# A selective scan in a twelve-stage decoder: four batches one after another, against four prepared in bulk and 64 states in one sequence

## The reference, cut to what matters

```python
xi = silu(conv3(u @ Win + b_in))            # depthwise convolution over time, three taps
z  = silu(u @ Wg + bg)
dt = softplus(xi @ Wdt + bdt)               # B=4, T=512, D=128
Bm, Cm = xi @ Wb + bb, xi @ Wc + bc         # 16 states
dA  = exp(dt[..., None] * A)
dBx = dt[..., None] * Bm[:, :, None, :] * xi[..., None]
h_t = dA_t * h_{t-1} + dBx_t                # for each batch, channel, state
y_t = sum over states of h_t * C_t
out = (y * z) @ Wout + bout                 # added to the residual x
```

## Time and profile before

| | us |
|---|---|
| median of 3 runs | 3147.62 (3141.78 to 3148.28) |
| profiled execution | 3148.16, its span 3146.4 |
| PE, DVE, ACT, POOL busy | 2411.6, 1811.8, 1239.4, 534.3 |
| the phase `l1_attn` in the span | 449.4 to 706.8 |

### The profile page before, as it was taken

How to read it: one execution, slowest core, us unless ns; L and a number is a source line. 1 busy time by engine, 2 the same in 40 slices (tenths; PEclk the granted TensorE clock), 3 DMA queues, 4 the chain that set the end, 5 groups by cost and what they waited for, 6 DMA issues and landing times. The chain is left out here.

```text
span 3146.4 us, 40958 instructions
## 1 busy us (share of the span) xinstructions
PE 2411.6 (77%) x12416; PEld 1417.6 (45%) x12416; DVE 1811.8 (58%) x4431; ACT 1239.4 (39%) x2575; POOL 534.3 (17%) x509
## 2 busy tenths in 40 slices
PE   6763976666768998699688888775888879578587
PEld 4653642224623323366344444453444456557454
DVE  4666347778855576444544444345666643745777
ACT  2442342224344454322466666523444422223212
POOL 0410000003310000000455555342000000043100
PEclk7875977777879999799799999877999989688799
DMA  0000000001010000000322222000000000100000
GB/s 32 31 6 0 1 5 0 0 0 44 1 55 1 0 0 0 0 0 0 97 69 68 68 68 68 22 31 24 1 0 0 0 1 0 56 23 1 1 1 14
DMA packets 19876, 61.81 MB, mean 20 GB/s; under 512 B 4928, under 2 KB 4928, under 8 KB 18592
## 3 DMA queue, kind: packets, MB, share of 16 engines
q1 hardware_dynamic: 19488, 59.53, 6.0%
q10 hardware_dynamic: 256, 0.68, 0.1%
HBM read 42.37 MB, written 1.05 MB: 14 GB/s over the span
## 5 line engine op out<-in xcount | busy, mean ns | idle before, releaser
L689 DVE TENSOR_REDUCE MF<-P 128x1 f32<-128x512 f32 (+3 forms) x512 | 282.3, 587 | 97.4 <-PE P L479 53.3
L824 ACT ACTIVATE PT<-P 128x512 f32<-128x512 f32 (+3 forms) x512 | 244.2, 516 | 232.5 <-PE P L496 123.0
L2318 PE MATMUL P<-XT,W 128*128 x424 | 221.0, 618 | 63.4 <-ACTq L2352 63.4
L2394 DVE SCALAR_TENSOR_TENSOR X<-P,WE,X 128x128 f32 x576 | 162.5, 344 | 167.0 <-PE P L2335 162.0
L2335 PEld LDWEIGHTS P<-W,e_h 128*128 128x128 f32 (+1 forms) x1952 | 220.7, 191 | 61.1 <-issue 53.2
L2335 PE MATMUL P<-W,e_h 128*128 128x128 f32 (+1 forms) x1952 | 227.8, 278 | 3.3 <-DVE X L2394 3.3
L1286 POOL TENSOR_TENSOR d_e<-d_e,d_rc 128x512 f32<-128x512 f32 (+3 forms) x256 | 178.2, 723 | 223.1 <-DVE d_rc L1193 223.0
L2363 ACT ACTIVATE e_g<-P 128x512 f32<-128x512 f32 x148 | 88.4, 597 | 310.5 <-PE P L2318 310.5
L496 PE MATMUL P<-QA,KA 128*128 128x512 bf16 (+3 forms) x512 | 180.2, 358 | 32.6 <-ACT PT L824 12.7
L479 PE MATMUL P<-KA,QA 128*128 128x512 bf16 (+3 forms) x512 | 182.2, 362 | 28.3 <-ACT KA L808 15.1
L541 PE MATMUL P<-PT,VA 128*32 128x512 f32 (+3 forms) x1024 | 195.8, 518 | 0.0
(11 more groups left out here) (359 smaller groups left out, 4635.5 us busy)
## 6 DMA issues: line engine op xcount, KB each, us to landing
d_bt<-in_alibi SPq DMA_DIRECT2D x32, 512.0 KB, 3.7
d_moved<-d_raw SPq DMA_DIRECT2D x256, 64.0 KB, 2.0
W<-in_w_L_xattn SPq DMA_DIRECT2D x1, 4291.0 KB, 14.1
W<-in_w_L_ffn SPq DMA_DIRECT2D x1, 3333.0 KB, 11.1
W<-in_w_L_ffn SPq DMA_DIRECT2D x1, 3155.0 KB, 10.2
W<-in_w_L_attn SPq DMA_DIRECT2D x1, 2636.0 KB, 11.6
W<-in_w_L_ffn SPq DMA_DIRECT2D x1, 2310.0 KB, 9.0
W<-in_w_L_ffn SPq DMA_DIRECT2D x1, 1744.0 KB, 6.9
```

The lines of the kernel that those rows point to most:

```text
L689: last = v.tensor_reduce(col, src, AX.X, ALU.max, negate=True)
L824: a.activation(k.PT[0:self.kp, h % self.slots, t, N - w:N], src, ACT.Exp, scale=self.scale).then_inc(s("exp_done"), 1)
L2318: pe.matmul(P[:, PG + j % 2, :], w["w1"][:, col:col + 128], x, start=True, stop=True).then_inc(s("gate"), 1)
L2394: last = v.scalar_tensor_tensor(x, y, k.WE[:, bass.ds(c * 4 + t, 1), e], x, ALU.mult, ALU.add)
```

## The change: what it does

Nothing outside `l1_attn` changes but the packing of `bout`, which becomes a row repeated over the 128 partitions. In the phase:

- The loop over batches is gone; every buffer of the preparation has one part per batch, and the four batches are prepared stage by stage before the first state.
- The bias and copy of the first product move from DVE to ACT (`conv_in`). dt and dt*x move from DVE to GpSimd (`delta`). `bout` is added to all of `X` at once by GpSimd; the products with ones are gone.
- The 64 states (16 of each batch) are one sequence. The product `inp` is split: ACT copies the spread B row with its bias from PSUM to `BE`, and GpSimd multiplies `BE` by dt*x into `BX`. DVE keeps the scan and `out`.
- `DA` gets three parts. B rows are spread two states ahead of C rows.
- The product with z comes 4 states after the last one of its batch, the product with Wout after 6, the addition to `X` after 9; the sum over states has two PSUM banks in turn.

The core of the diff (removed lines are those printed above):

```diff
+            def add_state(m):
+                b, n = m // NS, m % NS
+                pe.wait_ge(s("hc"), m + 1)
...
+                pe.matmul(P[:, BANK_Y + b % 2, :], k.ident[:], HC[:, m % 2, :], start=n == 0, stop=n == NS - 1).then_inc(s("summed"), 1)
...
+            for m in range(ALLS + AFTER_OUT + 1):
+                if m + 2 < ALLS:
+                    b_row(m + 2)
+                if m < ALLS:
+                    c_row(m)
+                if 0 <= m - 2 < ALLS:
+                    add_state(m - 2)
+                if m >= AFTER_OUT and (m - AFTER_OUT) % NS == 0 and m >= NS:
+                    out((m - AFTER_OUT) // NS - 1)
 
         @block.scalar
...
+            def b_row(m):
+                a.wait_ge(s("b_full"), m + 1)
+                if m >= 2:
+                    a.wait_ge(s("bx"), m - 1)
+                a.activation(BE[:, m % 2, :], P[:, BANK_B + m % 2, :], ACT.Identity, bias=w["bb"][:, m % NS:m % NS + 1]).then_inc(s("be"), 1)
+
+            def decay(m):
+                if m % NS == 0:
+                    a.wait_ge(s("dt"), m // NS + 1)
+                if m >= 3:
+                    a.wait_ge(s("scan"), m - 2)
+                a.activation(DA[:, m % 3, :], DT[:, m // NS, :], ACT.Exp, scale=w["a"][:, m % NS:m % NS + 1]).then_inc(s("da"), 1)
...
+            for b in range(B):
+                delta(b)
+            for m in range(ALLS):
+                b_row(m)
+                decay(m)
+
+        @block.gpsimd
+        def _(g):
...
+            g.tensor_tensor(k.X[:], k.X[:], w["bout"].unsqueeze(1).to_broadcast([128, TILES, D]), ALU.add).then_inc(s("offset"), 1)
+
+            def delta(b):
+                g.wait_ge(s("re"), b + 1)
+                g.wait_ge(s("ab"), 2 * b + 2)
+                g.tensor_tensor(DT[:, b, :], RE[:, b, :], AB[:, b, :], ALU.add).then_inc(s("dt"), 1)
+                g.wait_ge(s("dt"), b + 1)
+                g.tensor_tensor(DTX[:, b, :], DT[:, b, :], XS[:, b, :], ALU.mult).then_inc(s("dtx"), 1)
+
+            for b in range(B):
+                delta(b)
+            g.wait_ge(s("dtx"), B)
+            for m in range(ALLS):
+                g.wait_ge(s("be"), m + 1)
+                if m >= 2:
+                    g.wait_ge(s("scan"), m - 1)
+                g.tensor_tensor(BX[:, m % 2, :], BE[:, m % 2, :], DTX[:, m // NS, :], ALU.mult).then_inc(s("bx"), 1)
 
         @block.vector
...
+            def scan(m):
+                v.wait_ge(s("da"), m + 1)
+                v.wait_ge(s("bx"), m + 1)
+                if m >= 2:
+                    v.wait_ge(s("hc"), m - 1)
+                v.tensor_tensor_scan(H[:, m % 2, :], DA[:, m % 3, :], BX[:, m % 2, :], 0.0, ALU.mult, ALU.add).then_inc(s("scan"), 1)
+
+            def out(m):
+                v.wait_ge(s("c_full"), m + 1)
+                v.wait_ge(s("scan"), m + 1)
+                if m >= 2:
+                    v.wait_ge(s("summed"), m - 1)
+                v.scalar_tensor_tensor(HC[:, m % 2, :], P[:, BANK_C + m % 2, :], w["bc"][:, m % NS:m % NS + 1], H[:, m % 2, :],
+                                       ALU.add, ALU.mult).then_inc(s("hc"), 1)
...
+            for m in range(ALLS + AFTER_ADD + 1):
+                if m < ALLS:
+                    scan(m)
+                if 0 <= m - 1 < ALLS:
+                    out(m - 1)
+                if m >= NS and m % NS == AFTER_Z:
+                    gated(m // NS - 1)
+                if m >= NS and m % NS == AFTER_ADD:
+                    add(m // NS - 1)
```

More of the change, by code:

```diff
@@ L1975, in _ @@
             w_ready(pe)
[L1976 to L1981, removed]
-                pe.wait_ge(s("xs"), b + 1)
[L1983 to L2003, removed]
@@ L2004, in _, with out @@
+            def out(b):
                 pe.wait_ge(s("yz"), b + 1)
-                pe.wait_ge(s("m_free"), 3 * b + 3)
+                if b == 0:
+                    pe.wait_ge(s("rest"), B)
+                else:
+                    pe.wait_ge(s("added"), b)
                 for t in range(QT):
-                    o = P[:, PM, 128 * t:128 * (t + 1)]
-                    pe.matmul(o, YZ[:, 128 * t:128 * (t + 1)], w["wout"], start=True, stop=False)
-                    last = pe.matmul(o, k.ones[0:1, 0:128], w["bout"], start=False, stop=True)
@@ L2010, in _ @@
-                last.then_inc(s("m_full"), 1)
+                    last = pe.matmul(P[:, BANK_OUT, 128 * t:128 * (t + 1)], YZ[:, b % 2, 128 * t:128 * (t + 1)], w["wout"], start=True, stop=True)
+                last.then_inc(s("out_full"), 1)
+            conv_in(0)
+            conv_in(1)
+            gate(0)
+            gate(1)
+            conv_in(2)
+            conv_in(3)
+            delta(0)
+            gate(2)
+            gate(3)
+            delta(1)
+            rows(0)
+            rows(1)
@@ L2014, in _, with conv_in @@
             w_ready(a)
-            a.sem_inc(s("z_free"), 1)
-            with a.Fori(0, B) as b:
-                a.wait_ge(s("conv"), b + 1)
[L2018 to L2022, removed]
+            def conv_in(b):
+                a.wait_ge(s("in_full"), b + 1)
+                if b == 0:
+                    a.wait_ge(s("edges"), 1)
+                a.activation(XC[:, b, 1:N + 1], P[:, BANK_A + b % 2, :], ACT.Identity, bias=w["bin"]).then_inc(s("xc"), 1)
@@ L2023, in _ @@
                 a.wait_ge(s("abs"), b + 1)
-                a.activation(AB[:], AB[:], ACT.Exp, scale=-1.0).then_inc(s("ab"), 1)
+                a.activation(AB[:, b, :], AB[:, b, :], ACT.Exp, scale=-1.0).then_inc(s("ab"), 1)
                 a.wait_ge(s("ab"), 2 * b + 1)
[L2026 to L2030, removed]
+                a.activation(AB[:, b, :], AB[:, b, :], ACT.Ln, bias=1.0).then_inc(s("ab"), 1)
@@ L2034, in _ @@
             w_ready(v)
[L2035 to L2043, removed]
@@ new lines, in _ @@
+            for b in range(B):
+                conv(b)
+            for b in range(2):
+                positive(b)
+            for b in range(2):
+                rows(b)
+            for b in range(2, B):
+                positive(b)
+            for b in range(2, B):
+                rows(b)
+            for m in range(ALLS + AFTER_ADD + 1):
[7 more added lines that the diff above has]
+                    add(m // NS - 1)
```

184 lines of the change are left out of this document (120 added, 64 removed).

## The result

The kernel after takes 3098.36 us (median of 4 runs, 3087.09 to 3098.92) against 3145.76 (4 runs, 3141.78 to 3148.28): ratio 0.9839, 95% interval 0.9816 to 0.9862. A second set gave 3094.02 (5 runs, 3087.2 to 3098.48) against 3149.24, ratio 0.9825 (0.9811 to 0.9839). Forecast were 3092 and a range of 3068 to 3106: faster, and in the range.

A forecast was written before the change was run, and what follows sets the result against it. Bound per state: GpSimd's product and DVE's scan in turn. First scan's end 490.0, 63 periods of 2.43 (153.1), insertions 1, tail 6.4 end the phase at 650.5, 56.3 us less than 3148.16: 3092 us, range 3068 to 3106.

The forecast's parts named there:

- The clash: In the states: DVE's scan, with two SBUF inputs, and GpSimd's product exclude each other, so the scan waits.
- The period: Time per state in the sequence: 2.43 us against 2.63 before; chance 0.70 for 2.35 to 2.6.
- the hand-over: Between a scan's end and the start of GpSimd's next product: 0.08 us per state.
- the scan's rest: What the waiting scan still takes after GpSimd's product ends: 1.08 us per state.
- The preparation: Work ahead of the states, once instead of four times: first scan ends at 490.0, about 41 us into the phase.
- The insertions: Three products with z and three additions inside the sequence, mostly under the wait for GpSimd: 1 us in all.
- The tail: From the last scan to the end of the last addition: 6.4 us, against 8.6 before.
- PE: About 2.55 us per state at 1.2 GHz, half at 2.4; nothing taken, 8 us if all states ran low.
- The shared scan: Rival in the states: scan runs beside GpSimd's product, 1.99 us per state, 3066 us (halfway 2.2, 3077); chance 0.17.
- A held `out`: Rival in the states: `out` also waits for GpSimd, period 2.87 us, 3120 us; chance 0.10, shared with a dearer product.
- The full relay: Rival in the states: scan, `out` and product all wait in turn, 3.9 us per state, 3184 us; chance 0.03.
- the drains were hidden before: Rival between batches: preparations and tails already overlapped, so the change does less than it says; no size or separate chance.

The follow-up runs named there:

- psum_da: Changed kernel with decays written to two PSUM banks instead of SBUF, and products with Wout moved after the last state: 3063.69 us, ratio 0.9733 to the kernel before.
- h3_only: Changed kernel with a third buffer of H, so a scan no longer waits for the `out` in front of it: 3092.46 us, ratio 0.9826.
- pool_one: Changed kernel with GpSimd's product reading one repeated column of dt*x (states computed from a wrong factor): 3081.46 us, a single run.
- best: psum_da with softplus grouped by function on ACT, GpSimd's `bout` addition after its last product, later batches' dt and dt*x between states: 3064.85 us, ratio 0.9745.
- after_again: The changed kernel measured again with no edit: 3094.02 us, ratio 0.9825 to the kernel before.
- bulk_dve: Changed kernel, but DVE makes `inp` itself from PSUM as before, without ACT's copy and GpSimd's product: 3108.07 us, ratio 0.9871.
- bx3: Changed kernel with three buffers of `BX` instead of two, so GpSimd's next product can queue behind the running scan: 3085.4 us, ratio 0.9813.
- psum_h3: psum_da with a third buffer of H and nothing else: 3050.17 us, ratio 0.9695 to the kernel before.

## Why the prediction was right

**The clash, right.** The step that decided was that a scan with two SBUF inputs and GpSimd's product exclude each other. It was taken from products in another phase; no row showed a scan. psum_da, h3_only and pool_one show it for the scan: the wait goes when one input moves to PSUM, the end doesn't move with an earlier start, and the period falls by as much as GpSimd's product does.

**The period, 2.43 forecast and 2.49 found.** The term that was off is the hand-over: 0.08 us from the earlier trace rows, where DVE's instruction had 2 columns; behind a scan it is 0.14. Product (1.27) and the scan's rest (1.08) held. That is 63 x 0.062 = 3.9 us.

**The preparation: the end of the first scan forecast 40.8 us after the phase's start (490.0 - 449.2), found at 38.7.** The first Abs came 13.9 us after the start and not 16.2, which was the term that was off. GpSimd's addition, four convolutions of 2.1 and a Silu make 14.0 by the forecast's own terms; the other 2 us were put on the third convolution's wait for the Silu of the first, and that wait was 0.59. But the 14.0 is right by luck: in best, which has no addition there, the third convolution waits 2.26 us instead, the Silu of the first convolution comes 8.4 us after the start as in after, and so does the first Abs after 13.9. So the addition, which the forecast put on the path, is not on it. The four softplus took 17.8 (18.3 forecast), the rest up to the end of the first scan 7.0 (6.3).

**The insertions** were put at 1 us in all and cost nothing: the interval with one is 2.88, the next one 2.11, which is twice 2.49. They lie wholly under the wait for GpSimd. **The tail** was put at 6.4 and is 5.3 (6.9 in after_again): the wait for PE ahead of the addition fell from 3.69 to 1.25, more than by half. **PE** took nothing: the granted clock in the states was 0.91, before 0.79, nearer to the upper level of 2.4 GHz.

So the errors were -2.1 (to the end of the first scan), +3.9 (63 periods), -0.6 (mostly the last scan, which has no product beside it and is through in 1.23), -1 (the insertions) and -1.1 us (the tail), and the phase came out at 200.4 where 201.3 stood (650.5 - 449.2). The mechanism was right, but that the sum is so close is partly luck: terms of 1 to 4 us cancelled. The medians lie 6 and 2 us above the forecast and the profiled execution 5 below. The untouched stages, which the forecast took as they were in one profile and single ones of which differ by up to 4 to 6 us between profiles, are the likely reason; no run separates it.

**The rivals.** The shared scan (1.99 us per state, or 2.2 halfway) falls with the 2.49 of the timeline, and with h3_only, where an earlier start gave no earlier end. A held `out` (above 0.74) falls with the timeline: `out` runs beside the product's start at 0.72. The full relay (3.9) falls with it. That the drains were hidden before falls with bulk_dve: without the hand-over the phase was still 44.9 us shorter.

## What to carry to other kernels

Before work is handed from DVE to GpSimd, look at where the inputs of DVE's neighbouring instruction lie. If both are in SBUF and the order is fixed as it is here, the product's whole duration comes back in the period, as a wait that the profile books as busy time. Let ScalarE write one of the inputs to PSUM, if two banks can be freed: here that turned a gain of 12 us of phase into one of 41. What another buffer is worth depends on which wait ends last: a third `H` gave 0.1 us of phase while the scan stood behind GpSimd and 13.5 when nothing stood, and a third `BX`, which lets the product queue, gave 9.9. So remove the standing first, and compare an instruction's mean duration with the one that it has alone before reading an engine's busy share.

## What the runs showed of the hardware that was not expected

- A scan of 128x512 float32 takes the same time with one input in PSUM (1.21 to 1.22 us) as with both in SBUF and GpSimd idle (1.22 to 1.23).
- A tiny DVE product stands as long as a large one: in after, 96x32 bf16 with two SBUF inputs took 4.39 us beside GpSimd's addition of 4.52; in best, without the addition, it took 0.17. A copy with a single SBUF input can stand as well: in the split of rows of after it took 1.24 us beside GpSimd's product and 0.28 with GpSimd idle. So counting a neighbour's SBUF inputs is not enough for copies. Timelines:

```profile
447.26 4.52 POOL L2130 TENSOR_TENSOR X<-X,W 128x2048 f32<-128x2048 f32 x1
447.42 4.39 DVE L2153 TENSOR_TENSOR m_pick<-m_pick,identb 96x32 bf16<-96x32 bf16 x1
477.64 0.28 DVE L2183 COPY m_parts<-m_mid 32x512 bf16<-32x512 bf16 x1
480.68 1.24 DVE L2183 COPY m_parts<-m_mid 32x512 bf16<-32x512 bf16 x1
```

- With a product queued, scan and product alternate in 2.14 us, 0.35 less than where a semaphore opens the product; and the turn goes to the one that was issued first: an instruction more on DVE gave GpSimd two turns in a row (bx3).
- With DVE never waiting (psum_h3) the granted clock of TensorE was 1.00, its upper level, in 40 us of states (500 to 540), with PE busy for 32.4 of them; before it was 0.79, with 26.3 of 39.9.
